# A second set of scratch tiles for the odd half of each FFN output block (layer with linear attention and a ternary FFN, 8 cores)

## The reference

```python
x = x + layernorm(attn(layernorm(x)))        # linear attention, 16 heads, relu features
x = x + layernorm(ffn(layernorm(x)))

def tlin(x, w, s): return einsum('bsi,oi->bso', x, w) * s     # w ternary, s per output
def ffn(x):
    h = silu(tlin(x, w1, s1)) * tlin(x, w2, s2)   # 1024 -> 4096, twice
    h = gelu(tlin(h, h1, sh1))                    # 4096 -> 4096
    h = gelu(tlin(h, h2, sh2))                    # 4096 -> 4096
    return tlin(h, w3, s3)                        # 4096 -> 1024
```

## Time and profile before

| | us |
|---|---|
| median of 3 runs | 8320.38 |
| lowest, highest | 8319.91, 8392.85 |
| the profiled execution | 8320.38 |
| its span, slowest core (6) | 8318.8 |
| spans of the other cores | 8280.9 to 8309.6 |
| TensorE busy | 6417.5 (77%) |
| VectorE busy | 2172.4 (26%) |
| ScalarE busy | 1708.7 (21%) |

### The profile page before, as it was taken

How to read it: one execution, slowest core, us unless ns; L and a number is a source line. 1 busy time by engine, 2 the same in 40 slices (tenths; PEclk the granted TensorE clock), 3 DMA queues, 4 the chain that set the end, 5 groups by cost and what they waited for, 6 DMA issues and landing times.

```text
span 8318.8 us, 127042 instructions; the slowest of 8 cores (8280.9 to 8318.8 us)
## 1 busy us (share of the span) xinstructions
PE 6417.5 (77%) x52432; PEld 3009.5 (36%) x52432; DVE 2172.4 (26%) x3032; ACT 1708.7 (21%) x2637; POOL 208.7 (3%) x386
## 2 busy tenths in 40 slices
PE   6844456899995679999858444568999956799997
PEld 2311112455552234455323111224555512344553
DVE  2356533200013330000133565331001133200012
ACT  1211123211111331111112111232111123211111
POOL 0000000000000000000000000000000000000000
PEclk8766778999997889999977667789999978899998
DMA  3120022344442224444331200123334412243443
GB/s 67 38 49 21 11 51 41 62 77 76 77 97 61 41 46 77 77 77 77 77 76 34 53 21 11 51 41 72 77 76 78 94 54 41 56 77 75 78 76 78
DMA packets 97206, 503.36 MB, mean 61 GB/s; under 512 B 7360, under 2 KB 15744, under 8 KB 48512
## 3 DMA queue, kind: packets, MB, share of 16 engines
q0 software_dynamic: 68224, 394.56, 25.9%
q1 hardware_dynamic: 28416, 100.67, 3.4%
HBM read 856.11 MB, written 33.55 MB: 107 GB/s over the span
## 4 chain that ended last, share of the span: by engine, by line
PE 63%; DVE 18%; ACT 7%; DMA 7%; issue 4%; DVEq 1%; ACTq 0%; POOL 0%; SPq 0%; POOLq 0%
PE psb L77 51%; DVE ltmp L99 7%; ACT ltmp L88 5%; DMA wc<-w_t 4%; PE psb L79 4%; PE psb L56 4%; PE psb L72 4%; DVE normsb L127 3%; DVE a L113 2%; DMA xbf<-x 1%; DVE xa L99 1%; DMA xpr<-xp_hbm 1%; ACT sq L88 1%; DVE y L99 1%; DVE xp L99 1%
## 5 line engine op out<-in xcount | busy, mean ns | idle before, releaser
L77 PE MATMUL psb<-a,wc 64*128 64x512 bf16 x10240 | 2225.9, 378 | 50.7 <-DVE a L113 27.1
L79 PE MATMUL psb<-a,wc 64*128 64x512 bf16 x10240 | 2226.1, 378 | 0.0
L99 DVE TENSOR_TENSOR ltmp<-ltmp,psb 128x512 f32<-128x512 f32 x1152 | 791.4, 687 | 4203.9 <-ACT ltmp L88 4182.7
L77 PE MATMUL psb<-b,wc 64*128 64x512 bf16 x8192 | 1773.8, 377 | 12.0 <-ACT b L88 12.0
L79 PE MATMUL psb<-b,wc 64*128 64x512 bf16 x8192 | 1773.8, 377 | 0.0
L88 ACT ACTIVATE ltmp<-psb 128x512 f32<-128x512 f32 x1216 | 726.2, 597 | 3953.2 <-PE psb L79 3499.1
L77 PE MATMUL psb<-xnw,wc 64*128 64x512 bf16 x4096 | 993.0, 396 | 558.4 <-DMA wc<-w_t 400.7
L77 PEld LDWEIGHTS psb<-a,wc 64*128 64x128 bf16 x10240 | 965.2, 94 | 1161.9 <-issue 73.0
L72 PE MATMUL psb<-warm,onestat 128*1 128x512 bf16 x1664 | 524.4, 469 | 763.7 <-ACT sq L88 263.0
L77 PEld LDWEIGHTS psb<-b,wc 64*128 64x128 bf16 x8192 | 771.1, 94 | 854.0 <-issue 19.6
L79 PE MATMUL psb<-xnw,wc 64*128 64x512 bf16 x4096 | 996.1, 397 | 0.0
(11 more groups left out here) (110 smaller groups left out, 3392.1 us busy)
## 6 DMA issues: line engine op xcount, KB each, us to landing
wc<-h_t POOLq DMA_DIRECT2D x256, 1024.0 KB, 8.5
wc<-w_t POOLq DMA_DIRECT2D x96, 1024.0 KB, 9.0
xb<-x SPq DMA_DIRECT2D x16, 2048.0 KB, 10.3
xpr<-xp_hbm SPq DMA_DIRECT2D x16, 2048.0 KB, 12.8
xp_hbm<-xp SPq DMA_DIRECT2D x8, 2048.0 KB, 10.7
out<-outt SPq DMA_DIRECT2D x8, 2048.0 KB, 7.3
xbf<-x POOLq DMA_DIRECT2D x8, 1024.0 KB, 10.5
WA<-wk POOLq DMA_DIRECT2D x2, 2048.0 KB, 25.3
```

Source lines behind the costliest of these rows:

```text
L77: self.h.matmul(outA, lhsT[0:64, :], rhs[0:64, :], start=start, stop=stop, tile_position=(0, 0))
L79: ins = self.h.matmul(outB, lhsT[64:128, :], rhs[64:128, :], start=start, stop=stop, tile_position=(64, 0))
L99: ins = self.h.tensor_tensor(out, in0, in1, op)
```

## The change

Three tiles of 128 x 512 float32 are added: `ltmpB`, `ltmp2B`, `ltmp3B`, at 138, 140 and 142 KB above the base of the big region, just above `xp`. In the w1/w2, h1/h2 and w3 stages the units of half 1 use them, those of half 0 the old ones. The guard gets a second counter, `st["ltmp_veB"]`, for the units of half 1. The squares ahead of the last layer norm wait for both counters. Number, order, engines and shapes of all instructions stay the same. The core of the diff:

```diff
+        ("ltmpB", [128, TT], F32, B0 + 138 * KB),
+        ("ltmp2B", [128, TT], F32, B0 + 140 * KB),
+        ("ltmp3B", [128, TT], F32, B0 + 142 * KB),
...
+        "ltmp_veB": 0,
...
                 pe_w2 = p.c["pe"]
+                lt0, lt2, lt3 = (("ltmp", "ltmp2", "ltmp3") if h == 0 else
+                                 ("ltmpB", "ltmp2B", "ltmp3B"))
+                lkey = "ltmp_ve" if h == 0 else "ltmp_veB"
                 p.w("S", "pe", pe_w1)
-                p.w("S", "ve", st["ltmp_ve"])
-                p.act(t["ltmp2"][:, :], ps[w1A][:, :], AF.Identity)
+                p.w("S", "ve", st[lkey])
+                p.act(t[lt2][:, :], ps[w1A][:, :], AF.Identity)
                 bank_consumed(w1A, "se")
                 se_i1 = p.c["se"]
                 p.w("V", "se", se_i1)
-                p.tt(t["ltmp3"][:, :], t["ltmp2"][:, :], ps[w1B][:, :], ALU.add)
+                p.tt(t[lt3][:, :], t[lt2][:, :], ps[w1B][:, :], ALU.add)
                 bank_consumed(w1B)
                 ve_s1 = p.c["ve"]
                 p.w("S", "ve", ve_s1)
-                p.act(t["ltmp"][:, :], t["ltmp3"][:, :], AF.Silu,
+                p.act(t[lt0][:, :], t[lt3][:, :], AF.Silu,
                       scale=t["s1"][:, oc:oc + 1])
...
-                p.stt(al(oc, h), t["ltmp3"][:, :], t["s2"][:, oc:oc + 1],
-                      t["ltmp"][:, :], ALU.mult, ALU.mult)
-                st["ltmp_ve"] = p.c["ve"]
+                p.stt(al(oc, h), t[lt3][:, :], t["s2"][:, oc:oc + 1],
+                      t[lt0][:, :], ALU.mult, ALU.mult)
+                st[lkey] = p.c["ve"]
...
+                lt0, lt2 = ("ltmp", "ltmp2") if h == 0 else ("ltmpB", "ltmp2B")
+                lkey = "ltmp_ve" if h == 0 else "ltmp_veB"
                 p.w("S", "pe", pe_h)
-                p.w("S", "ve", st["ltmp_ve"])
-                p.act(t["ltmp"][:, :], ps[bA][:, :], AF.Identity)
+                p.w("S", "ve", st[lkey])
+                p.act(t[lt0][:, :], ps[bA][:, :], AF.Identity)
...
         p.w("S", "ve", st["ltmp_ve"])
+        p.w("S", "ve", st["ltmp_veB"])
```

More of the change, by code:

```diff
@@ L234, in build_program @@
     ]
-    need = max(B0 + 2 * NHC * W * 2, B0 + 138 * KB)
+    need = max(B0 + 2 * NHC * W * 2, B0 + 144 * KB)
     assert need <= ARENA, ("big region overflow", need, ARENA)
@@ L847, in emit_ffn_window @@
                 p.w("S", "pe", pe_w2)
-                p.act(t["ltmp2"][:, :], ps[w2A][:, :], AF.Identity)
+                p.act(t[lt2][:, :], ps[w2A][:, :], AF.Identity)
                 bank_consumed(w2A, "se")
@@ L852, in emit_ffn_window @@
                 p.w("V", "se", se_i2)
-                p.tt(t["ltmp3"][:, :], t["ltmp2"][:, :], ps[w2B][:, :], ALU.add)
+                p.tt(t[lt3][:, :], t[lt2][:, :], ps[w2B][:, :], ALU.add)
                 bank_consumed(w2B)
-                p.stt(al(oc, h), t["ltmp3"][:, :], t["s2"][:, oc:oc + 1],
-                      t["ltmp"][:, :], ALU.mult, ALU.mult)
-                st["ltmp_ve"] = p.c["ve"]
+                p.stt(al(oc, h), t[lt3][:, :], t["s2"][:, oc:oc + 1],
+                      t[lt0][:, :], ALU.mult, ALU.mult)
+                st[lkey] = p.c["ve"]
         st["wslice_done"][k1] = p.c["pe"]
@@ L885, in emit_ffn_window @@
                 p.w("V", "se", se_i)
-                p.tt(t["ltmp2"][:, :], t["ltmp"][:, :], ps[bB][:, :], ALU.add)
+                p.tt(t[lt2][:, :], t[lt0][:, :], ps[bB][:, :], ALU.add)
                 bank_consumed(bB)
-                st["ltmp_ve"] = p.c["ve"]
-                p.w("S", "ve", st["ltmp_ve"])
-                p.act(dstf(oc, h), t["ltmp2"][:, :], AF.Gelu,
+                st[lkey] = p.c["ve"]
+                p.w("S", "ve", st[lkey])
+                p.act(dstf(oc, h), t[lt2][:, :], AF.Gelu,
                       scale=t[sc_t][:, oc:oc + 1])
@@ L914, in emit_ffn_window @@
             pe_f = p.c["pe"]
+            lt0 = "ltmp" if h == 0 else "ltmpB"
+            lkey = "ltmp_ve" if h == 0 else "ltmp_veB"
             p.w("S", "pe", pe_f)
-            p.w("S", "ve", st["ltmp_ve"])
-            p.act(t["ltmp"][:, :], ps[bA][:, :], AF.Identity,
+            p.w("S", "ve", st[lkey])
+            p.act(t[lt0][:, :], ps[bA][:, :], AF.Identity,
                   scale=t["s3"][:, oc:oc + 1])
@@ L921, in emit_ffn_window @@
             p.w("V", "se", se_i)
-            p.stt(fl(oc, h), ps[bB][:, :], t["s3"][:, oc:oc + 1], t["ltmp"][:, :],
+            p.stt(fl(oc, h), ps[bB][:, :], t["s3"][:, oc:oc + 1], t[lt0][:, :],
                   ALU.mult, ALU.add)
             bank_consumed(bB)
-            st["ltmp_ve"] = p.c["ve"]
+            st[lkey] = p.c["ve"]
         st["wslice_done"][k] = p.c["pe"]
```

## The result

| | before | after |
|---|---|---|
| the profiled execution, us | 8320.38 | 8195.47 |
| its span, slowest core | 8318.8 (core 6) | 8193.9 (core 3) |
| mean of the eight spans | 8299.4 | 8179.7 |
| median of the four lowest runs, us | 8318.2 | 8192.8 |

In more than half of the ten runs of each kernel the cores of one die or of both ran at a lower granted clock and for longer, for which the forecast had no term, so that the medians over all ten, 8481 us after (outside the forecast range of 8168 to 8243) and 8468 us before, say nothing on the change; the ratio, the table and the times in this document are of the other runs, called *counted runs*, unless it says otherwise.

The account below looks back on a forecast made before the run. The prediction took the ScalarE/VectorE chain in w1/w2 to set the pace in mid-slab, with TensorE stopping for PSUM banks. 32 slabs x 4.1 us = 131 us off 8320 gave 8189 us, range 8168 to 8243.

Parts of the forecast that it names:

- What bounds the kernel, and where the change acts: In w1/w2, ScalarE and VectorE take turns, 4.87 us a unit, and TensorE stops for PSUM banks; savings come there.
- The cycle of 4.05 us: In w1/w2, one unit's ScalarE and VectorE steps would take 4.05 us instead of 4.87, 0.82 us less.
- rival B: In w1/w2, copy and add reading PSUM together disturb each other: 8285 us fully in turns, 8221 at 0.2 us a cycle; chance 0.10.
- Slab ends: At w1/w2 slab ends the 12.2 us weight wait stays; at h1 the transfer replaces the product as releaser, so all 32 slabs count.
- h1, h2, w3: In these stages ScalarE waits 4.58 us of each unit for TensorE, so the second scratch set gains and costs 0.
- 4.1 us a slab: Saving for each w1/w2 slab, five cycles of 0.82 us; ends of the range 3.8 and 4.5 us.
- TensorE's own floor: In a w1/w2 slab, TensorE's time without stops, slow restart included: 31.0 us, 4.2 less than 35.25, so it may bind first.
- The sum: Over the whole kernel, 32 slabs times 4.1 us give 131 us less, so 8189 us.
- The low side of the range: Whole kernel: 4.5 us a slab gives 8176 us, a few less if core 6's first-stage landing falls from 16.24 towards 12.2; 8168.
- C: In w1/w2, weight landings growing to 16.24 us take back 113 of the 131 us: 8302 us; chance 0.08.
- D: In w1/w2, weight landings of 17.89 us lose 160 us, making the kernel slower: 8349 us; chance 0.03.
- E: In w1/w2, the change doesn't act because TensorE hasn't the next unit's products ready: 8320 us; chance 0.03.

Follow-up runs that it names:

- the six kernels in the table: GpSimd memsets ahead of weights: kernel before with none, four (8320.38, 8382.04 us); changed kernel with none, two, four, six (8195.47, 8215.75, 8245.6, 8289.25 us).

## Why the prediction was right, and where it was wrong

- **What bounds the kernel, and where the change acts.** Right. The gain is in w1/w2 alone (the kernels with the change only in w1/w2 and only outside it).
- **The cycle of 4.05 us.** Right: 4.06 measured, with every gap as worked out.
- **Two engines on PSUM at once (rival B).** It costs nothing: on core 3, 193 copies lie for more than 0.4 us beside a VectorE instruction that reads PSUM, and take 597 ns in the median and 602 at most; the adds take 687 ns, as before. This is what the Trainium skill ("PSUM — Partial Sum Buffer", "Specifications (TRN2)") states for different banks, and the trace agrees.
- **Slab ends.** Right: the waits for weights stayed at 95.4 us in the stage above, and at h1 the transfer took the product's place (8.74 us against 9.03).
- **h1, h2, w3.** Right, 0 within the measurement.
- **4.1 us a slab.** This is the step of the prediction that failed: the mechanism held, the size of this term did not. It was 3.74 over all cores. What was left out is that TensorE's own floor, restart included, takes back part of what the chain gives. The prediction computed this floor once, 31.0 us, for a slab with 13 low pairs, and found it 4.2 below that slab's 35.25. It then took 4.1 off the *mean* slab of 34.8, which gives 30.7, and that is below the floor just computed. The kernel before had only 10 or 11 low pairs in most slabs of the last stage, and they cost it nothing as long as the chain was the pace; a reader of the restart in the earlier trace rows alone could not see this. Measured: 31.12 us in the slab above. From 34.8 that is 3.7, the mean found.
- **Where the difference went.** In the mean of the eight cores TensorE's stops within the 32 slabs (distances of pairs beyond 0.2155 us, behind the restart) fell from 143.5 to 10.7 us, 4.15 a slab, so what the chain gave is what was forecast. Against it stand the low pairs, which rose from 10.5 to 11.7 a slab in the mean of all 32 (1.2 x 0.2155 x 32 = 8 us), longer pauses for weights (1.5 us in all), and some 3 us outside of both. That the low pairs would rise was not foreseen.
- **The sum.** 131 forecast; 119.7 in the mean of the cores and 124.9 on the slowest core of the profiled executions. The slowest core gained more than the mean: before it was core 6, which lost time to slow landings in its first stage (16.24 in the earlier trace rows) and whose span fell by 144 us, to 8174.5. The low side of the range had named this. So 8195 beside 8189 owes part of its closeness to this second effect, which makes up 5 of the 11 us that the first is short; that part is luck.
- **What would show it.** TensorE's waits for VectorE were to fall under 8 us a stage: 0.4. The stage was to fall from 371 to 338 us: from the first matmul to the end of the last one the stage that starts at 5228.38 takes 341.4. One sign of being wrong came: more than 13 pairs at the lower level after a restart, with 14 in four of the last seven slabs of the last w1/w2 stage (core 3).
- **Rivals C, D and E** did not come. TensorE's pause for weights is 13.89 us in the mean of all cores, after 13.84. Behind the first w1/w2 stage no landing in the chains of waits of these stages is longer than 12.9 us; in the first one those of core 3 take 12.5 to 15.1, and a single one in another of its stages takes 18.28. ScalarE's early copies are taken up.
- **The reason given for the price** was right but wider than it needed to be. The prediction said that the copy waited for the product, and priced the removal of that wait; it left open whether the second set was necessary. It wasn't: the last reader of the overwritten tile is the second add.
- **Two slips in the arithmetic.** A and half of B and C come to 0.85, not 0.86, and 8221 + 21 is 8242, not 8243. Nothing hangs on either.

## What to carry to other kernels

When one engine waits to overwrite a scratch tile, look for the last instruction that reads this very tile; a counter that is taken after a later one makes the engines take turns, and moving the line costs no memory. After removing a wait, compare the remaining chain with the floor of the engine that it feeds, slab by slab and with the restart included: here they met, so that a chain shortened once more gave only 11 us, while taking the pauses for weights away gave 336 us (8195 to 7859). And the two belong together: a pause that lets a chain drain hides its price, so that the same change is worth 125 us with the pauses and 204 to 211 without.

## What the hardware showed that was not expected

After a pause of 13.4 to 20.2 us TensorE runs at its lower level (1.2 GHz, pairs 0.427 us apart) for 6 to 14 pairs, some 2.5 to 5.9 us, and the number differs between slabs that are equal in every instruction. In some stages it stays near a value (10, 8 or 14) or changes between two (8 and 13); in others it climbs slab by slab and falls back, as in the third stage of the changed kernel's core 1 with 14 13 14 6 9 10 11 13. What decides it is left open by these runs; the moment of the restart moves it, the rhythm of the slabs alone doesn't set it. A change that alters the length of a pause can so win or lose time by this alone. The means of the six kernels in the table lie between 9.6 and 12.1 pairs, and 2.5 x 0.21 x 28 = 15 us is an estimate of what that is worth here, before any waits for the chain are taken off.

One memset of 128x512 float32 on GpSimd took 0.524 us, and four in a row took 2.45, with the DMA issue right behind them.
